# Reordering the first batch of a two-layer fp32 kernel: the third context's load, the second scan, the key product's second pair, and two VectorE orders

## The reference

```
# layer 1: projection plus a decaying scan over the context, picked by patch
n = layernorm(x)
h = rmsnorm(n, g_res) @ W_in.T + b_in
s[i] = a * s[i-1] + c * rmsnorm(ctx, g_init)[i, :512]     # i over the rows of ctx
x = x + h + s[plug]                                       # plug: row index from the running sum of the patch lengths
# layer 2: channel mixing with a shift by one row
y  = layernorm(x);  y_prev = y shifted down by one row
xr = mu_r * y + (1 - mu_r) * y_prev;   xk = mu_k * y + (1 - mu_k) * y_prev
r  = sigmoid(xr @ W_r.T);   k = square(relu(xk @ W_k.T))
x  = x + r * (k @ W_v.T)
```

## Time and profile before

| | |
|---|---|
| median of three runs | 763.65 us (763.37 to 764.11) |
| the profiled execution | 761.57 us, span 760.0 us |
| granted TensorE clock, mean | 0.991 |
| TensorE busy | 745.4 us (98%) |
| VectorE busy | 586.7 us (77%) |
| ScalarE busy | 405.5 us (53%) |
| GpSimd busy | 171.7 us (23%) |
| chain that ended last, by engine | PE 92%, DMA 4%, POOL 1%, DVE 1%, issue 1% |

### The profile page before, as it was taken

One profiled execution on the slowest core, in us unless ns is written; L12 is line 12 of the kernel. 1 busy time (PEld: TensorE's weight loads), 2 busy tenths in 40 slices (PEclk: granted clock), 3 DMA queues, 4 the chain that ended last, 5 costly groups with the idle time before them and its releaser, 6 DMA issues.

```text
span 760.0 us, 11067 instructions
## 1 busy us (share of the span) xinstructions
PE 745.4 (98%) x3432; PEld 616.0 (81%) x3433; DVE 586.7 (77%) x1063; ACT 405.5 (53%) x666; POOL 171.7 (23%) x163
## 2 busy tenths in 40 slices
PE   7988999999999999999999999999999999999998
PEld 5866788888888888888888888888888888888887
DVE  7888996887869778696876879778696977867462
ACT  4177354754545556453754545465364655544860
POOL 6441230313131031312113131121312113130000
PEclk9999999999999999999999999999999999999999
DMA  8667371726446272633716355281634627240011
GB/s 308 172 194 187 117 200 56 206 98 154 138 112 180 69 185 104 159 135 93 205 54 162 129 137 166 79 222 56 153 125 109 193 67 192 96 125 14 1 56 56
DMA packets 51453, 100.02 MB, mean 132 GB/s; under 512 B 5134, under 2 KB 5390, under 8 KB 51388
## 3 DMA queue, kind: packets, MB, share of 16 engines
q1 hardware_dynamic: 41900, 82.46, 31.6%
q0 software_dynamic: 9216, 16.78, 13.4%
q10 hardware_dynamic: 288, 0.27, 0.1%
HBM read 64.26 MB, written 21.76 MB: 113 GB/s over the span
## 4 chain that ended last, share of the span: by engine, by line
PE 92%; DMA 4%; POOL 1%; DVE 1%; issue 1%; ACT 0%; SPq 0%; DVEq 0%; POOLq 0%
PE bank L561 29%; PE bank L562 29%; PE bank L563 29%; PE bank L697 3%; POOL ring L505 1%; DMA ring<-s_rows,patch_now 1%; DMA xt<-in_L_ffn_W_r 1%; PE bank L791 1%; DMA ring<-s_rows,patch_of 1%; DMA above<-u 1%; DMA s_rows<-scanned 1%; PE bank L770 0%; DMA ctx_rows<-in_ctx 0%; DMA lens<-in_mask_BxS_if 0%; POOL rs_a L459 0%
## 5 line engine op out<-in xcount | busy, mean ns | idle before, releaser
L505 POOL DMA_INDIRECT ring<-s_rows,patch_now x60 | 99.9, 1665 | 228.8 <-DMA s_rows<-scanned 198.1
L1136 DVE SCALAR_TENSOR_TENSOR scratch<-turned,cols,scratch 128x512 f32<-128x512 f32 x128 | 94.4, 748 | 32.0 <-ACT scratch L862 21.9
L1003 DVE TENSOR_TENSOR xr_lo<-scratch,xr_hi 128x512 fp32r<-128x512 f32 x124 | 85.1, 688 | 39.8 <-ACT xr_hi L813 38.9
L813 ACT ACTIVATE turned<-bank 128x512 f32<-128x512 f32 x64 | 33.1, 604 | 131.1 <-PE bank L697 131.1
L561 PE MATMUL bank<-wi_hi,xt_hi 128*128 128x512 f32 x256 | 101.9, 398 | 0.0
L561 PE MATMUL bank<-xk_hi,wk_hi 128*128 128x512 f32 x256 | 100.0, 391 | 1.0 <-DVE xk_lo L1003 0.6
L563 PE MATMUL bank<-wi_hi,xt_lo 128*128 128x512 f32 x256 | 100.6, 393 | 0.0
L562 PE MATMUL bank<-wi_lo,xt_hi 128*128 128x512 f32 x256 | 100.5, 393 | 0.0
L561 PE MATMUL bank<-wr_hi,xr_hi 128*128 128x512 f32 x256 | 100.1, 391 | 0.0
L562 PE MATMUL bank<-wr_lo,xr_hi 128*128 128x512 f32 x256 | 100.0, 391 | 0.0
L563 PE MATMUL bank<-wr_hi,xr_lo 128*128 128x512 f32 x256 | 99.8, 390 | 0.0
(11 more groups left out here) (148 smaller groups left out, 1267.1 us busy)
## 6 DMA issues: line engine op xcount, KB each, us to landing
ring<-in_x SPq DMA_DIRECT2D x16, 1024.0 KB, 5.2
out<-gate SPq DMA_DIRECT2D x63, 256.0 KB, 2.1
xt<-in_x_turned SPq DMA_DIRECT2D x14, 1024.0 KB, 7.2
above<-scanned SPq DMA_DIRECT2D x42, 224.0 KB, 2.7
ctx_rows<-in_ctx SPq DMA_DIRECT2D x15, 512.0 KB, 5.9
s_rows<-scanned SPq DMA_DIRECT2D x15, 256.0 KB, 2.5
above<-u SPq DMA_DIRECT2D x14, 224.0 KB, 2.7
gate<-in_L_xattn_W_in SPq DMA_DIRECT2D x4, 256.0 KB, 3.5
```

Of the source, the lines that this page charges most:

```text
L505: pool.indirect_dma_start(ring[b.slot][:, t, :], None, s_rows[:, :], bass.IndirectOffsetOnAxis(ap=rows, axis=0), compute_op=ALU.add).then_ ...
L813: return nc.scalar.activation(to, of, ACT.Copy)
L1003: return nc.vector.tensor_tensor(to, whole, high, ALU.subtract)
L1136: nc.vector.scalar_tensor_tensor(scratch[:, 2 + i % 2, :], turned[:, c, 1:S + 1], cols[:, 1 + which, c:c + 1], scratch[:, i % 2, :], ALU.m ...
```

## The change

Five orders change, all of them in the first batch; no operation is added or left out.

1. SyncE loads the third context when the first two gathers of batch 1 have landed, not all four.
2. VectorE adds the first tile of batch 0 (`add_x`) and takes its statistics ahead of the low part of the second half of batch 1's x turned.
3. ScalarE splits the first chunk of W_r not ahead of the turned copies but behind `carry(b, 0)`; `u_high` of batch 1 moves from there to behind the first high copy of xr. VectorE's `weight_lo(WR, 0, 1)`, `u_low`, `mix_low(nxt, 0)` and `scan_out(new)` move accordingly: `u_low` goes behind `mix_low(nxt, 0)`, and `scan_out` behind `mix_low(nxt, 1)`.
4. TensorE's scan of batch 1 (and the `far` branch) moves from ahead of the gate product of batch 0 into it, behind its first three products (tiles 0 to 2 of chunk 0); the fourth tile's chunk 0, which shares the bank with the scan, moves behind chunk 1 of the other three.
5. In the first key product, banks 2 and 3 are computed one after the other, each over all chunks, and no longer side by side.

```diff
--- before.py
+++ after.py
@@ -402,7 +402,8 @@
                                      gate[:, T - 1, half_tile(h)]).then_inc(half_stored[h], 16)
 
             store_scan(Batch(0, 1))
-            rows_added(sp, Batch(0, 1))
+            for t in range(T // 2):
+                reached(sp, dep_added[t], Batch(0, 1), 16, 16)
             reached(sp, far_over, Batch(0, 1), 1, 1)
             load_ctx(Batch(0, 2))
 
@@ -614,8 +615,13 @@
 
                 order = [(t, c) for t in range(T) for c in range(C)]
                 if is_first(b):
-                    order = [(t, c) for c in range(C) for t in range(T)]
+
+                    order = [(t, c) for c in range(2) for t in range(T - 1)] + [(T - 1, 0), (T - 1, 1)]
+                    order += [(t, c) for c in range(2, C) for t in range(T)]
                 for t, c in order:
+                    if is_first(b) and (t, c) == (0, 1):
+                        scan(b.plus(1))
+                        far(b.plus(1))
                     if c == 0:
                         reached(pe, gated, b.plus(-1), T, t + 1)
                     if t == 0:
@@ -633,17 +639,17 @@
             def first_key_product(b):
 
 
-                for pair in ((0, 1), (2, 3)):
-                    for c in range(C):
+                order = [(m, c) for c in range(C) for m in (0, 1)] + [(m, c) for m in (2, 3) for c in range(C)]
+                for m, c in order:
+                    if m == 0:
                         pe.wait_ge(w_lo_ready[WK], c + 1)
                         reached(pe, mix_lo_ready, b, 2 * C, C + c + 1)
-                        for m in pair:
-                            if c == 0:
-                                reached(pe, x2_ready, b.plus(1), T, m + 1)
-                            last = product(bank[m][:, :], wt_hi[WK][:, c, tile(m)], wt_lo[WK][:, c, tile(m)],
-                                           xk_hi[:, c, :], xk_lo[:, c, :], c == 0, c == C - 1)
-                            if c == C - 1:
-                                last.then_inc(k_done, 1)
+                    if c == 0:
+                        reached(pe, x2_ready, b.plus(1), T, m + 1)
+                    last = product(bank[m][:, :], wt_hi[WK][:, c, tile(m)], wt_lo[WK][:, c, tile(m)],
+                                   xk_hi[:, c, :], xk_lo[:, c, :], c == 0, c == C - 1)
+                    if c == C - 1:
+                        last.then_inc(k_done, 1)
 
             def key_product(b):
 
@@ -746,8 +752,6 @@
                 turn(b.plus(-1))
 
                 reached(pe, yt_ready, b.plus(-1), T, T)
-                scan(b)
-                far(b)
 
             def sum_limbs():
 
@@ -872,8 +876,7 @@
                             act.wait_ge(zero_ready, 1)
                         carry(b, 0)
                     if is_first(b) and i == 0:
-
-                        u_high(b.plus(1))
+                        weight_hi(WR, 0, 1)
                     elif i + 1 < 2 * C:
                         carry(b, i + 1)
                     which, c = mix_row(b, i)
@@ -886,6 +889,7 @@
                         reached(act, v_done, b.plus(-1), T, T)
                     copy((xr_hi, xk_hi)[which][:, c, :], scratch[:, 2 + i % 2, :]).then_inc(mix_hi_ready, 1)
                     if is_first(b) and i == 0:
+                        u_high(b.plus(1))
                         carry(b, 1)
                     if is_first(b) and i < C - 1:
                         weight_hi(WR, i + 1, i + 2)
@@ -960,7 +964,6 @@
 
                     reached(act, far_over, nxt, 1, 1)
                     squares_c(new)
-                    weight_hi(WR, 0, 1)
                     turned_out(nxt)
                 if nxt.exists(B) and not is_last(nxt) and not is_first(nxt):
                     turned_out(nxt)
@@ -1235,9 +1238,9 @@
             def iteration(b):
                 nxt, new = b.plus(1), b.plus(2)
                 if is_first(nxt):
-                    x_lo(new, 1)
                     add_x(nxt, 0)
                     statistics_b(nxt, 0)
+                    x_lo(new, 1)
                     add_x(nxt, 1)
                     statistics_b(nxt, 1)
                     statistics_a(new, 2)
@@ -1252,15 +1255,15 @@
                     norm_b(nxt, 0, T - 1)
                     norm_b(nxt, T - 1, T)
                     scan_input(new)
-                    weight_lo(WR, 0, 1)
                     stats_a(new, T)
                     mix_next(nxt, 0)
+                    weight_lo(WR, 0, 1)
+                    mix_low(nxt, 0)
                     u_low(new)
-                    mix_low(nxt, 0)
                     mix_next(nxt, 1)
-                    scan_out(new)
                     weight_lo(WR, 1, 2)
                     mix_low(nxt, 1)
+                    scan_out(new)
                     mix_next(nxt, 2)
                     weight_lo(WR, 2, 3)
                     mix_low(nxt, 2)
```

## The result

| | before | after |
|---|---|---|
| median of 20 runs each | 763.18 us | 767.76 us |
| ratio after/before, 95% interval | | 1.0065 (1.0051 to 1.0079) |
| profiled execution, span | 761.57, 760.0 us | 766.25, 764.7 us |

The change makes the kernel slower, by 5.0 us (0.0065 of 763.18; one run of each kernel, 1072.2 and 839.75 us, was in a slow state and is left out of the ratio). The prediction said slower, and its 765.8 us was too low; its range ended at 767.6. The profiled execution lost 4.7 us of span; 3.7 of them are lost by the end of TensorE's last wait in the start-up.

The account below looks back on a forecast made before the run. TensorE bounds the kernel, so only its waits before 76.88 us count. Roads of +2.1 and +2.4 us were taken as +2.2: 761.57 to 763.8 us profiled, 765.8 us as median; range 763.0 to 767.6 us.

Parts of the forecast that it names:

- The turn 0.28 sooner: First addition ahead of x turned's low part: TensorE's turn of batch 1 starts at 40.62, not 40.90, gaining 0.28 us.
- that case: First gather of batch 0 landing only at 32.23: low part ends at 34.9, TensorE stalls 1.1 us in the projection.
- the `above` transfer's term: Road to the first shifted addition through u (+2.5) and its 4.63 us DMAs: +2.4 us, less without a context load ahead.
- The loads collide: Rival: context's load takes near 7.0 us, ScalarE waits 2.0, x turned and above follow; about +3.5, 767.2 us; chance 0.10.
- the forecast's other road: VectorE's own way to the first shifted addition: 3.2 us late minus 1.07 us of waits, +2.1 us.
- The context sooner: Third context's load starts 0.9 us sooner, lands at 65.6 or 69.4; in the first case VectorE's 1.07 us of waits go.
- the sign of the collision: Check in the changed profile: ScalarE still waiting for the context would mean the loads collide.
- The clock: TensorE restarts at half clock after a long wait, matmuls at 0.63 us or more; each such restart costs about 1.7 us.
- the rival of the shorter pause: Rival: TensorE's last wait is one of 2.3 us and the clock stays up; +0.5, 764.3 us; chance 0.20.
- The key order: Key product's banks 2 and 3 one after the other: bank 2 done 2.0 us sooner, effect zero, bounds 0 and 0.6.
- The gather sooner: Rival: batch 1's first gather lands by 59.0, VectorE at +2.1, after the waits +1.0; 764.7 us; chance 0.12.
- the forecast's +2.2: Sum taken for the first shifted addition, from 75.53 to 77.7, and the value product, from 76.88 to 79.1.

Follow-up runs that it names:

- k9: Kernel before with only the new order of W_r's first copy, u_high, u_low and the mix; scan ahead of the gate product, scan_out in its old place; ratio 1.0005.
- k11: Kernel before with batch 1's scan inside the gate product behind three products, scan_out behind mix_low(nxt, 1), W_r and u_low in old order; ratio 1.0045.
- k6: Kernel before with only batch 0's first addition and statistics moved ahead of x turned's low part; ratio 1.0007.
- k3: Changed kernel with SyncE issuing the first step's two moves into above ahead of the loads of x and x turned; ratio to before 1.0041.
- k4: Changed kernel with the third context's load again waiting for all four gathers; ratio to before 1.0071.
- k5: Kernel before with only the third context's load waiting for two gathers instead of four; ratio 0.9998.
- k7: Kernel before with only banks 2 and 3 of the first key product computed one after the other; ratio 0.9990.
- k8: Kernel before with VectorE's far branch right behind scan_out and the third context loaded without waiting for any gather; ratio 0.9993.
- k12: k8 with banks 2 and 3 one after the other and the context's load held until the scan's store has landed; ratio to before 0.9995.
- k1: Changed kernel with the late scan and the new W_r and u_low orders undone; ratio to before 1.0024.
- k15: Kernel before with context behind two gathers, key banks in turn, above moves ahead of x, W_r's first copy behind carry(b, 0) and u_high; 760.66 us, ratio 0.9977.
- k16: Kernel before with only W_r's first copy moved behind carry(b, 0) and u_high, and key banks 2 and 3 one after the other; ratio 0.9991.
- k2: Kernel before with only the scan inside the gate product and the new orders around W_r's first copy; ratio 1.0050.
- k10: k2 with the scan behind one product of the gate product instead of three; ratio to before 1.0029.

## Why the prediction was wrong

**The direction and the first half were right.** The gate product starts at 46.70 (said 46.55), `scan_out` at 51.28 (51.1) with 1.89 us of idle VectorE ahead of it (1.5 or more), xr's last low part at 55.38 (55.2), the first gather at 54.77 (54.6), and the additions stand behind the gathers: 59.62 with a wait of 0.33 (60.1), TensorE waiting 0.43 and 1.69 us for `ring` in banks 0 and 1 (1 to 2, so the first was less). `u` is at +2.12 (+2.5). k9 to k11 show the mechanism that was named: what the scan is late, the value product is late.

**The turn 0.28 sooner** was wrong: the first gather hadn't landed when VectorE came (1.39 us), x turned's low part was late, and TensorE stood for 1.08 us at 33.73. That I had said 1.1 for that case is luck: the gather landed at 31.07 and not at 32.23, and TensorE asked at 32.65 and not at 33.8. The turn is at 40.88 where it was at 40.90, but the two executions differ in the clock from 14 to 24 us (1.00 after, 0.66 before). Against profiles with the same clock part 2 makes the turn 0.3 to 0.9 us later (k6 above), so with the 0.28 that was forecast as a gain the term is off by 0.6 us or more.

**The step that failed is the `above` transfer's term**: "u (69.43, +3.2 - 0.69 = +2.5) and its DMAs of 4.63 us, which landed 0.1 us before VectorE wanted them: +2.4, less if no context load runs ahead of the loads of x", and with it the 0.10 that I gave to the rival *The loads collide*, whose +3.5 us at the value product was nearly what came (+3.69). VectorE would have reached the shifted addition at 77.55 (79.22 - 1.67), +2.0, which is the +2.1 of the forecast's other road. The rest up to +3.69 is the wait for the move. The term let the move land a fixed time behind `u` (and its 4.63 us is the row of the 16 KB, not of the 224 KB). It lands behind x turned instead, at 79.2 and not at 75.4, +3.8 us, while `u` is at +2.12. "Less" had the wrong sign: the context's load beside the gathers took 6.50 us, not 3.18, the fourth gather beside it 7.6 and not 5.6, and the loads of x, which wait for that gather, started at 68.97 and not at 64.22. The Trainium skill, DMA: Bandwidth & Descriptors, "Issuing engines are not separate DMA queues", says that transfers interleave on the same 16 engines whichever engine issues them; the trace agrees (SyncE's load 6.50 against 3.18, GpSimd's fourth gather 7.6 against 5.6 us). k3 shows the loads of x as the cause of the move's delay: with the moves ahead of x, 1.65 us less at the last wait.

**The context sooner** thus bought nothing. ScalarE still waited for it, for 1.80 us, which the prediction named as the sign of the collision; the 1.07 us of VectorE's waits became 0.20 and 0.38, so half was gained there and more than that lost in `above`. k4 has the same time without part 1, k5 shows none alone.

**The clock** behind the last wait was at half again, 0.63 us a matmul up to 84.0, as said; the rival of the shorter pause fell, since the pause was 3.87 us and not 2.3. (That rival's time should read 764.15, 763.65 + 0.5, and not 764.3.) **The key order** at nothing was right (k7 0.9990). **The gather sooner**: it landed at about 59.6, not by 59.0.

**Behind 80.57** the changed profile is another 1.0 us longer (684.1 us from there to the end of the span, 683.1 before), for which the prediction had no term. That it is the change's isn't shown: k7, k8 and k12, which are no slower than before and had the same clock from 76 to 90 us (0.88), have 684.0, 683.9 and 683.9. TensorE's one wait there is the 0.38 at 445.45. VectorE pauses longer than before ahead of two mixing steps (3.41 against 2.17 us near 276, 3.84 against 2.98 near 412), but k7 pauses 3.46 and 3.52 there. Of the 2.8 us between the forecast's +2.2 and the measured +5.0, 1.5 are the `above` term, 0.6 or more is the turn by these profiles (the changed one hides it by its better clock), and the rest stays open.

## What to carry to other kernels

A load freed of a wait is not earlier by what it waited: look at what is in flight where it now runs, and at what then stands in front of the next small, urgent transfer; here the urgent move of 240 KB belonged ahead of 2 MB of loads, and then the next move stands beside them: look one step further before the gain is counted. When an operation that feeds a long road (scan, store, gather, addition) is put behind filler work of its own engine, the road is late by that work even though the engine stays busy. A gap in front of an instruction is only usable by work whose own inputs are already there; the profile shows a landing only where something waited for it.

## What the runs showed of the hardware

- A 512 KB load took 3.15 to 3.35 us alone, 3.1 in k12, where the first gather was issued 0.8 us behind it, and 5.7 (k3) to 7.26 (k1) beside two gathers. The fourth gather beside it took 7.0 to 8.5 us, without it 5.2 to 5.7.
- A 224 KB move that SyncE issued 2.9 to 6.0 us behind a 1 MB load landed 0.3 to 0.6 us behind that load in 15 of 16 profiles; issued ahead of it, it took 2.6 us (k3, k15).
- TensorE's granted clock from 14 to 24 us, ahead of every edit, was 1.00, 0.83, 0.66 or about 0.50 in different profiled executions. What is lost there doesn't come back by the end: the profiles of k7, k8 and k16, with 0.50 and no slower by their medians, end TensorE's last start-up wait 1.6 to 1.8 us later than that of before (0.66) and have spans of 762.2 to 762.5 us against 760.0.
- The same pause has two outcomes for the clock. Behind a last wait of 2.31 us it fell to half in k2 (matmuls at 0.59 to 0.63 us until 85.18) and in k7, and stayed at full in k9 and k10 (1.00 from 76 to 90); behind 2.16 us it stayed up in k15, behind 2.18 us it fell in k3 (0.88 in the same stretch).
- The 256 KB store took 2.0 us in sixteen of these profiles and 3.1 in the two (k8, k12) in which VectorE's branch was moved up behind `scan_out`; why isn't known.
